# Dynamic convolution in a four-layer kernel: the orders of TensorE, VectorE and ScalarE laid out anew

## The chip, the cores and the metric

One core of one Trainium2 chip runs the whole program. The metric is the device time of one execution in microseconds (us), the median of three runs. The profile shows one further execution, with its own time.

## The reference

Four layers follow one another on `x` (16 samples, 64 channels, 64 x 64), each fed with a group-normalised copy and added to its input. Only the first is touched by the change, a dynamic convolution:

```python
g = jnp.mean(x, axis=(2, 3))
h = jax.nn.relu(g @ w1.T + b1)
alpha = jax.nn.softmax(h @ w2.T + b2, axis=-1)
weff = jnp.einsum('bk,koihw->boihw', alpha, experts)
beff = jnp.einsum('bk,ko->bo', alpha, bias)
...
x = x + _L0_conv_ref(_gn(x), ...)
x = x + _L1_conv_ref(_gn(x), ...)
x = x + _L2_conv_ref(_gn(x), ...)
x = x + _L3_conv_ref(_gn(x), ...)
```

Each sample has its own 3 x 3 weights: four experts mixed by a softmax over a small network of the sample's channel means. The other layers are two sets of directional sweeps and one attention with a local part.

## The kernel before

`dyn_conv` handles one sample after another. A sample lies in `raw` (four buffers) with image rows of even and odd number on the two halves of the partitions; it is convolved in four pieces (`CH` = 4) of 512 columns. For fp32 accuracy both operands are split into a high and a low part: `xz_hi`, `xz_lo` (two buffers each) and `w_hi`, `w_lo`. A piece is 18 products (L604): 12 of `xz_hi` with both weight parts, in two blocks of six (`products_high`), and six of `xz_lo` with `w_hi` (`products_low`). A sample has 72 products.

While sample n is convolved, the weights of sample n+1 are made, and the result of n-1 is normalised. Who does what:

- VectorE: `input_stats` (L662, four pieces), `aggregate` (L311, L668) and `squares` (L672 to L674) give the moments; `group_var` (L679 to L684, L348 to L350) turns the group mean that TensorE made into a variance and the first guess of its inverse root; `gate_mean` (L697), `gate_hidden` (L702), `softmax_in` (L707 to L709), `mixing_weights` (L713 to L715); `mix` (L720 for expert 0, L722 for the other three, L727 for the added input), `low_weights` (L731); `remainder` (L736), which makes a half of `xz_lo`; `result_stats` (L743) of each evacuated piece, `effective_bias` (L746 to L748) and `result_affine` (L691).
- ScalarE: `centre` (L525) makes a half of `xz_hi`, `evacuate` (L532) adds a finished piece to its bias and writes it to `raw`, `hidden` (L537), `exps` (L541), `high_weights` (L545), and `to_slot` (L551): two moves of a quarter of the normalised result into `S` a call.
- TensorE: besides the products, `group` (L589) averages moments over channel groups (for the input, INP, and the result, RES), `hid` (L593) and `logits` (L598) are the two layers of the small network.
- GpSimd: the inverse root, eleven small steps for the input and eleven for the result (`newton_rsqrt`). SyncE: loads of samples and stores of results; the load of sample n+4 waits for the store of n and its four moves to `S`.

The order on each engine is the order of the code in `sample` of that engine's block; nothing reorders it. An engine waits where its next instruction's semaphore is not there, and all behind it waits too. The waits that matter here:

```python
def products_high(n, q, u, blk):
    if blk == 0:
        if q == 0:
            pe.wait_ge(w_ready, n + 1)
```
```python
def group(n, c):
    pe.wait_ge(me_ready[c], n + 1)
```
```python
def gate_hidden(m):
    dve.wait_ge(h_ready, m + 1)
```

`w_ready` comes from `low_weights`, `me_ready` from `squares`, `h_ready` from `hidden`. `walk` runs `sample` for n = 0 and 1, a loop of three turns of four samples, and two more.

## Time and profile before

| what | value |
|---|---|
| median of 3 runs | 3129.11 us (3128.0 to 3129.72) |
| the profiled execution's own time | 3132.45 us |
| its span | 3130.7 us |
| busy: TensorE, VectorE, ScalarE, GpSimd | 88%, 69%, 44%, 9% |
| dynamic convolution | 0 to about 429 us of the span |

The shares are means over four layers. The change concerns the first 429 us alone, and only what is read there bears on it. The profile gives the time of every instruction, the granted clock of TensorE (1.0 is the full 2.4 GHz, 0.5 is 1.2 GHz), and what ended an engine's idle time. A time ahead of an instruction is its start in us from the span's start.

### The profile page before, as it was taken

The page shows a single profiled execution, that of the slowest core. Times are in us where ns is not written, and L with a number is a line of the kernel's source. Part 1 is how long each engine was busy: PE and PEld are TensorE (multiplying, and loading weights), DVE is VectorE, ACT ScalarE, POOL GpSimd, SP SyncE. Part 2 cuts the span into 40 slices and gives each one's busy share as a digit, 9 for nine tenths or more (in the row PEclk, how much of TensorE's full clock was granted, in tenths as well). Part 3 has the DMA queues.
Part 4 walks back from the last instruction along what each step waited for, and adds up shares of the span by engine and source line. Part 5 has one row for each costly group of instructions (what it writes and reads, how often), then busy time and mean ns, then how long its engine had stood idle before and what let it go on. Part 6 is the DMA issues. An engine that isn't in the chain of part 4 may idle for free. (4 is left out here: it accounts for less than half of the span.)

```text
span 3130.7 us, 71818 instructions
## 1 busy us (share of the span) xinstructions
PE 2747.3 (88%) x25712; PEld 2482.8 (79%) x25712; DVE 2172.1 (69%) x5174; ACT 1363.0 (44%) x2113; POOL 288.4 (9%) x801
## 2 busy tenths in 40 slices
PE   5888879999999999917969998878999999999791
PEld 3666669999999999913447777758999999999791
DVE  7888846666666666687018888886666666666865
ACT  3766642246632222236436666643225662222120
POOL 1112110000000000045000101010000000000602
PEclk9899989999999999958979999998999999999795
DMA  4334230000000000087054877856000000000758
GB/s 89 81 90 99 67 124 0 0 0 0 0 0 0 0 0 0 0 233 198 1 87 73 120 104 102 116 73 107 0 0 0 0 0 0 0 0 0 121 94 127
DMA packets 735622, 164.89 MB, mean 53 GB/s; under 512 B 728209, under 2 KB 728849, under 8 KB 730641
## 3 DMA queue, kind: packets, MB, share of 16 engines
q1 hardware_dynamic: 608928, 136.86, 22.7%
q10 hardware_dynamic: 126576, 26.41, 5.4%
q8 instruction: 81, 1.33, 0.2%
q14 instruction: 37, 0.30, 0.0%
HBM read 96.13 MB, written 67.11 MB: 52 GB/s over the span
## 5 line engine op out<-in xcount | busy, mean ns | idle before, releaser
L269 PE MATMUL L_conv<-L_x_hi,L_w_hi 128*128 128x256 f32 x5040 | 1251.0, 283 | 46.5 <-DVE L_w_lo L236 28.7
L269 PE MATMUL L_conv<-L_x_hi,L_w_lo 128*128 128x256 f32 x5040 | 1249.5, 283 | 0.0
L156 ACT ACTIVATE L_row_b<-S,L_bias 128x256 f32 (+1 forms) x1008 | 514.2, 510 | 1168.9 <-DVE L_x_hi L210 1158.0
L269 PEld LDWEIGHTS L_conv<-L_x_hi,L_w_hi 128*128 128x128 f32 x5040 | 958.7, 190 | 49.5 <-issue 28.9
L269 PEld LDWEIGHTS L_conv<-L_x_hi,L_w_lo 128*128 128x128 f32 x5040 | 957.0, 190 | 0.0
L220 DVE SCALAR_TENSOR_TENSOR S<-L_conv,L_neg_bias,L_row_b 128x256 f32 x1008 | 487.7, 484 | 517.5 <-PE L_conv L273 516.7
L273 PE MATMUL L_conv<-L_x_lo,L_w_hi 128*128 128x256 f32 x5040 | 771.3, 284 | 4.9 <-DVE L_x_lo L212 4.8
L273 PEld LDWEIGHTS L_conv<-L_x_lo,L_w_hi 128*128 128x128 f32 x5040 | 677.7, 190 | 7.4 <-DVE L_x_lo L212 7.4
L212 DVE TENSOR_TENSOR L_x_lo<-S,L_x_hi 128x256 fp32r<-128x256 f32 x1016 | 455.3, 448 | 34.7
L210 DVE TENSOR_SCALAR L_x_hi<-S 128x256 fp32r (+1 forms) x1016 | 316.7, 312 | 35.3
L604 PE MATMUL dc_conv<-dc_xz_hi,dc_w_hi 128*128 128x512 f32 x384 | 171.3, 446 | 6.5 <-DVE dc_w_lo L731 6.5
L604 PE MATMUL dc_conv<-dc_xz_hi,dc_w_lo 128*128 128x512 f32 x384 | 166.2, 433 | 0.0
L160 ACT COPY S<-S (+1 forms) x252 | 156.2, 620 | 7.3 <-DVE S L220 2.8
L1690 POOL TENSOR_TENSOR fs_buf<-fs_buf,S 128x1024 f32<-128x1024 f32 x21 | 67.8, 3267 | 888.5 <-DVE S L220 786.2
L551 ACT ACTIVATE S<-dc_raw,dc_small 64x1024 f32 (+1 forms) x62 | 133.7, 2156 | 7.9 <-DVE dc_small L691 6.7
L604 PE MATMUL dc_conv<-dc_xz_lo,dc_w_hi 128*128 128x512 f32 x384 | 103.2, 404 | 0.0
L604 PEld LDWEIGHTS dc_conv<-dc_xz_hi,dc_w_hi 128*128 128x128 f32 x384 | 79.8, 208 | 26.1 <-DVE dc_w_lo L731 6.6
L945 PE MATMUL lp_taps<-S,lp_band 128*128 128x256 f32 x256 | 90.3, 435 | 9.6 <-ACT S L912 9.6
L338 POOL TENSOR_TENSOR lp_sq_pool<-lp_guess 128x1 f32<-128x1 f32 x48 | 9.3, 193 | 955.6 <-DVE lp_guess L350 953.0
L604 PEld LDWEIGHTS dc_conv<-dc_xz_hi,dc_w_lo 128*128 128x128 f32 x384 | 80.3, 209 | 19.3
L604 PEld LDWEIGHTS dc_conv<-dc_xz_lo,dc_w_hi 128*128 128x128 f32 x384 | 74.6, 194 | 20.3
L918 ACT ACTIVATE S<-lp_taps,lp_lb 128x256 f32<-128x256 f32 x128 | 57.8, 475 | 71.0 <-PE lp_taps L947 71.0
(177 smaller groups left out, 2896.4 us busy)
## 6 DMA issues: line engine op xcount, KB each, us to landing
dc_raw<-x SPq DMA_DIRECT2D x32, 512.0 KB, 6.6
x_scratch<-dc_raw SPq DMA_DIRECT2D x16, 1024.0 KB, 7.4
lp_xr<-x_scratch SPq DMA_DIRECT2D x16, 1024.0 KB, 7.0
x_scratch<-lp_xr SPq DMA_DIRECT2D x32, 512.0 KB, 7.7
at_res<-x_scratch SPq DMA_DIRECT2D x32, 512.0 KB, 10.5
x_scratch<-at_res SPq DMA_DIRECT2D x64, 256.0 KB, 5.3
fs_buf<-x_scratch SPq DMA_DIRECT2D x32, 512.0 KB, 6.7
at_G<-x_scratch ACTq DMA_DIRECT2D x56, 256.0 KB, 5.8
```

Of the source, the lines that this page charges most:

```text
L156: nc.scalar.activation(row_b[p][:, :, :], line(k, at_step(k, i), p), ACT.Identity, bias=bias[:, k:k + 1]).then_inc(row_b_ready[p], 1)
L160: nc.scalar.copy(*quarter(hj, *QUARTERS[q])).then_inc(act_moved, 1)
L210: nc.vector.tensor_scalar(inner(x_hi[p]), row, 1.0, None, ALU.mult).then_inc(hi_ready[p], 1)
L212: nc.vector.tensor_tensor(inner(x_lo[p]), row, inner(x_hi[p]).bitcast(F32), ALU.subtract).then_inc(lo_ready[p], 1)
L220: nc.vector.scalar_tensor_tensor(out=row, in0=conv[p][:, 0:NB * J].rearrange("p (j b) -> p j b", b=NB), scalar=neg_bias[:, k:k + 1], in1=r ...
L269: nc.tensor.matmul(out, w[:, k, s * P:(s + 1) * P], x_hi[p][:, s:s + J, :], start=(s == 0 and n == 0), stop=False)
L273: mm = nc.tensor.matmul(out, w_hi[:, k, s * P:(s + 1) * P], x_lo[p][:, s:s + J, :], start=False, stop=(s == NBLK - 1))
L551: nc.scalar.activation(dst, src, ACT.Identity, bias=shift, scale=scale).then_inc(s_done, 1)
L604: mm = nc.tensor.matmul(conv[q][:, :], part[:, at:at + P], x[:, q * CB + blk:q * CB + blk + CB, dw:dw + W], start=(first and dw == j == 0) ...
L918: nc.scalar.activation(column(every, slice(0, J), w, p), taps[g % 4][:, 0:J * NB].rearrange("p (i b) -> p i b", b=NB), ACT.Identity, bias= ...
L945: nc.tensor.matmul(out, bands.band0[:, w, :], column(every, slice(0, J), w, p), start=True, stop=False)
L1690: return eng.tensor_tensor(buf[:, :, :], buf[:, :, :], columns_of(self.S, item % B)[:, :, self.columns(item)], ALU.add)
```

## The change

Four things are changed in `dyn_conv`.

1. TensorE: the group average of the next input stands behind the first piece of a sample and no longer ahead of it; `hid` and `logits` come later in the products.
2. VectorE: within a sample, `remainder` of the second half is made in the sample that uses it, right after `effective_bias`; `remainder` of the first half stands between `mixing_weights` and the mixing; `gate_hidden` follows `gate_mean`. `mix` of expert 0 leaves VectorE.
3. ScalarE: it scales expert 0 into PSUM (`first_expert`), `centre` of the second half comes ahead of `exps`, and the moves to `S` are spread singly, the fourth into the next sample.
4. The start: the first mixing precedes the statistics of the second input; the experts are loaded by SyncE behind sample 0. The end: VectorE makes three of the last sample's moves, ScalarE one.

The diff, cut to its core: first `sample` of TensorE, then that of VectorE with its start, then `first_expert` and `sample` of ScalarE.

```diff
             def sample(t, k):
...
-                if not last:
-                    group(n + 1, INP)
                 products_high(n, 0, u, 0)
                 products_high(n, 0, u, 1)
                 products_low(n, 0, u)
                 if not last:
-                    hid(n + 1)
+                    group(n + 1, INP)
                 products_high(n, 1, u, 0)
                 if not first:
                     group(n - 1, RES)
+                products_high(n, 1, u, 1)
+                if not last:
+                    hid(n + 1)
+                products_low(n, 1, u)
+                products_high(n, 2, u, 0)
                 if not last:
                     logits(n + 1)
-                products_high(n, 1, u, 1)
-                products_low(n, 1, u)
...
             def sample(t, k):
                 if not last:
                     group_var(n + 1, INP, k + 1)
+                effective_bias(k)
+                remainder(n, k, 1)
                 if not first:
                     result_stats(n * CH - 1, (k - 1) % PER, CH - 1)
-                effective_bias(k)
-                if not first:
                     aggregate("result", RES)
                     squares(RES)
                 if not last:
                     gate_mean(n + 1, k + 1)
-                    remainder(n + 1, k + 1, 0)
                     gate_hidden(n + 1)
                 if not first:
                     group_var(n - 1, RES, k - 1)
...
                 result_stats(n * CH, k % PER, 0)
                 if not last:
                     mixing_weights(n + 1)
-                    for e in range(KE):
-                        mix(n + 1, (k + 1) % 2, e)
+                    remainder(n + 1, k + 1, 0)
                 if not first:
                     result_affine(n - 1, k - 1)
+                if not last:
+                    for e in range(1, KE):
+                        mix(n + 1, (k + 1) % 2, e)
                 result_stats(n * CH + 1, k % PER, 1)
                 if not last:
-                    remainder(n + 1, k + 1, 1)
                     low_weights(n + 1, (k + 1) % 2)
...
             gate_hidden(0)
+            softmax_in(0)
+            mixing_weights(0)
+            dve.wait_ge(ex_in, 2 * 16)
+            for e in range(1, KE):
+                mix(0, 0, e)
+            low_weights(0, 0)
             remainder(0, 0, 0)
-            softmax_in(0)
-            remainder(0, 0, 1)
...
+            def first_expert(m): 
+                act.wait_ge(weight_ready, m + 1)
+                nc.scalar.activation(w_mix, ex[0], ACT.Identity, scale=weight[:, 0:1]).then_inc(first_mixed, 1)
...
             def sample(t, k):
                 if not first:
                     evacuate(n * CH - 1, (k - 1) % PER, CH - 1, n - 1)
+                if not first and not second:
+                    to_slot(n - 2, (k - 2) % PER, 1, 1)
                 if not last:
                     centre(t, k + 1, 0)
                 evacuate(n * CH, k % PER, 0, n)
                 if not last:
                     hidden(n + 1)
+                    centre(t, k + 1, 1)
                     exps(n + 1)
-                    centre(t, k + 1, 1)
+                    first_expert(n + 1)
                 evacuate(n * CH + 1, k % PER, 1, n)
+                if not first:
+                    to_slot(n - 1, (k - 1) % PER, 0, 0)
                 if not last:
                     high_weights(n + 1, (k + 1) % 2)
                 if not first:
-                    to_slot(n - 1, (k - 1) % PER, 0)
+                    to_slot(n - 1, (k - 1) % PER, 0, 1)
                 evacuate(n * CH + 2, k % PER, 2, n)
                 if not first:
-                    to_slot(n - 1, (k - 1) % PER, 1)
+                    to_slot(n - 1, (k - 1) % PER, 1, 0)
```

TensorE, sample 1, from the end of sample 0's products. Before (L604 are products, L589 `group`, L593 `hid`, L598 `logits`):

```order
L604 MATMUL dc_conv<-dc_xz_lo,dc_w_hi 128x512 x6
L589 MATMUL dc_group<-dc_small,dc_avg 128x2
L604 MATMUL dc_conv<-dc_xz_hi,dc_w_hi 128x512
...
L604 MATMUL dc_conv<-dc_xz_lo,dc_w_hi 128x512 x6
L593 MATMUL dc_gate<-dc_small,dc_w1s 32x1
L604 MATMUL dc_conv<-dc_xz_hi,dc_w_hi 128x512
...
L589 MATMUL dc_group<-dc_small,dc_avg 128x2
L598 MATMUL dc_gate<-dc_small,dc_ones 128x4
```

And with the change (L619 products, L604 `group`, L608 `hid`):

```order
L619 MATMUL dc_conv<-dc_xz_lo,dc_w_hi 128x512 x6
L619 MATMUL dc_conv<-dc_xz_hi,dc_w_hi 128x512
...
L619 MATMUL dc_conv<-dc_xz_lo,dc_w_hi 128x512 x6
L604 MATMUL dc_group<-dc_small,dc_avg 128x2
L619 MATMUL dc_conv<-dc_xz_hi,dc_w_hi 128x512
...
L604 MATMUL dc_group<-dc_small,dc_avg 128x2
L619 MATMUL dc_conv<-dc_xz_hi,dc_w_hi 128x512
...
L608 MATMUL dc_gate<-dc_small,dc_w1s 32x1
L619 MATMUL dc_conv<-dc_xz_lo,dc_w_hi 128x512 x6
```

The first `group` (the next input's) has moved behind a whole piece of 18 products; the second (the last result's) has stayed six products behind the first piece, and `hid` now comes six products after it and no longer ahead of it.

VectorE, from the last guess step of the input's `group_var` on. Before:

```order
L350 TENSOR_SCALAR dc_small<-dc_small 128x1
L743 BN_STATS dc_bn<-dc_raw 128x6
L746 TENSOR_TENSOR dc_small<-dc_small 128x4
...
L674 TENSOR_TENSOR dc_small<-dc_small 128x1
L697 TENSOR_SCALAR dc_small<-dc_small 128x1
L736 SCALAR_TENSOR_TENSOR dc_xz_lo<-dc_raw,dc_small,dc_xz_hi 64x17x64 x2
L702 TENSOR_SCALAR dc_small<-dc_small 32x4
L679 COPY dc_small<-dc_group 128x2
```

And with the change (L752 `remainder`, L759 `result_stats`, L691 the end of `squares`, L714 `gate_mean`, L719 `gate_hidden`):

```order
L764 TENSOR_TENSOR dc_small<-dc_small 128x1
L752 SCALAR_TENSOR_TENSOR dc_xz_lo<-dc_raw,dc_small,dc_xz_hi 64x15x64 x2
L759 BN_STATS dc_bn<-dc_raw 128x6
...
L691 TENSOR_TENSOR dc_small<-dc_small 128x1
L714 TENSOR_SCALAR dc_small<-dc_small 128x1
L719 TENSOR_SCALAR dc_small<-dc_small 32x4
L696 COPY dc_small<-dc_group 128x2
```

Two instructions of `remainder` now stand ahead of the result's statistics, and none between `gate_mean` and `gate_hidden`.

## Rows read from the trace of the kernel before

**Rows 1.** Busy time and granted clock in two stretches of the dynamic convolution (columns in the first line).

```profile
core 0: us, PE busy (x) PEld busy (x) DVE busy (x) ACT busy (x) POOL busy (x), PEclk, DMA share, GB/s
100.00:200.00 100.00, 83.88 (x332) 64.29 (x330) 84.68 (x220) 70.36 (x66) 18.70 (x96) 0.91 0.37 85
200.00:300.00 100.00, 81.01 (x321) 61.89 (x320) 84.90 (x227) 71.00 (x67) 18.68 (x96) 0.93 0.36 84
```

**Rows 2.** Waits of TensorE between 60 and 380 us: in total, times, longest.

```profile
PE dc_group L589 <- DVE dc_small L674: 39.4, 13, 3.3
```

**Rows 3.** The tile of the mixed weights: count, ns min/median/max, first and last start.

```profile
L545 ACT CAST dc_w_hi<-dc_mixed x16: 799/802/804, 34.3 to 388.9; 128x768 fp32r<-128x768 f32 x16
L731 DVE TENSOR_TENSOR dc_w_lo<-dc_mixed,dc_w_hi x16: 956/958/960, 35.1 to 392.0; 128x768 fp32r<-128x768 f32 x16
```

**Rows 4.** VectorE in order of time, 51 to 56 us (start, us, line, operation).

```profile
54.19 0.96 DVE L731 TENSOR_TENSOR dc_w_lo<-dc_mixed,dc_w_hi 128x768 fp32r<-128x768 f32 x1
```

**Rows 5.** VectorE in order of time, one sample of the loop.

```profile
149.66 0.96 DVE L731 TENSOR_TENSOR dc_w_lo<-dc_mixed,dc_w_hi 128x768 fp32r<-128x768 f32 x1
...
154.34 0.14 DVE L679 COPY dc_small<-dc_group 128x2 f32<-128x2 f32 x1
...
157.37 0.69 DVE L743 BATCH_NORM_STATS2 dc_bn<-dc_raw 128x6 f32<-128x512 f32 x1 [1.88 <-ACT dc_raw L532]
...
159.16 0.27 DVE L697 TENSOR_SCALAR dc_small<-dc_small 128x1 f32<-128x1 f32 x1
159.70 2.73 DVE L736 SCALAR_TENSOR_TENSOR dc_xz_lo<-dc_raw,dc_small,dc_xz_hi 64x1088 fp32r<-64x1088 f32 x2 [0.28 <-ACT dc_xz_hi L525]
...
163.81 0.15 DVE L707 TENSOR_TENSOR dc_small<-dc_gate,dc_small 128x4 f32<-128x4 f32 x1
...
165.57 1.02 DVE L720 TENSOR_SCALAR dc_mixed<-S,dc_small 128x768 f32<-128x768 f32 x1
166.63 3.14 DVE L722 SCALAR_TENSOR_TENSOR dc_mixed<-dc_ex,dc_small,dc_mixed 128x768 f32<-128x768 f32 x3
...
170.41 0.69 DVE L743 BATCH_NORM_STATS2 dc_bn<-dc_raw 128x6 f32<-128x512 f32 x1
171.01 2.44 DVE L736 SCALAR_TENSOR_TENSOR dc_xz_lo<-dc_raw,dc_small,dc_xz_hi 64x960 fp32r<-64x960 f32 x2
173.49 0.96 DVE L731 TENSOR_TENSOR dc_w_lo<-dc_mixed,dc_w_hi 128x768 fp32r<-128x768 f32 x1
```

**Rows 6.** TensorE in order of time, the same sample and the next one's head.

```profile
153.87 0.38 PE L589 MATMUL dc_group<-dc_small,dc_avg 128*128 128x2 f32 x2 [2.81 <-DVE dc_small L674]
...
166.00 0.40 PE L604 MATMUL dc_conv<-dc_xz_hi,dc_w_hi 128*128 128x512 f32 x1
...
170.28 0.40 PE L604 MATMUL dc_conv<-dc_xz_hi,dc_w_hi 128*128 128x512 f32 x1
...
177.69 0.59 PE L589 MATMUL dc_group<-dc_small,dc_avg 128*128 128x2 f32 x2 [2.96 <-DVE dc_small L674]
178.15 0.77 PE L604 MATMUL dc_conv<-dc_xz_hi,dc_w_hi 128*128 128x512 f32 x1
...
183.41 1.63 PE L604 MATMUL dc_conv<-dc_xz_lo,dc_w_hi 128*128 128x512 f32 x6
```

**Rows 7.** The start: hidden layer of the first sample.

```profile
17.87 0.26 PE L593 MATMUL dc_gate<-dc_small,dc_w1s 128*32 128x1 f32 x2 [4.96 <-DVE dc_small L697]
19.46 0.25 ACT L537 ACTIVATE dc_small<-dc_gate,dc_small 32x1 f32<-32x1 f32 x1
```

**Rows 8.** The end of the stage: last convolution, its evacuation, the last moves.

```profile
413.54 1.58 PE L604 MATMUL dc_conv<-dc_xz_lo,dc_w_hi 128*128 128x512 f32 x6
416.54 0.69 ACT L532 ACTIVATE dc_raw<-dc_conv,dc_small 128x512 f32<-128x512 f32 x1
423.91 4.24 ACT L551 ACTIVATE S<-dc_raw,dc_small 64x1024 f32<-64x1024 f32 x2 [6.68 <-DVE dc_small L691]
423.91 2.33 DVE L823 TENSOR_SCALAR S<-dc_raw,dc_small 64x1024 f32<-64x1024 f32 x2
```

More of the change, by code:

```diff
@@ L288 @@
 HID = 32
-PER_LOOP = 34
+PER_LOOP = 32
 PER = 4
@@ L384, in dyn_conv @@
     logit, prob, alpha, bprod = small[:, 20:24], small[:, 24:28], small[:, 28:32], small[:, 32:36]
-    top, total, beff, gmean = small[:, 36:37], small[:, 37:38], small[:, 38:39], small[:, 39:40]
+    top, total, gmean = small[:, 36:37], small[:, 37:38], small[:, 39:40]
+    beff = [small[:, 76 + u:77 + u] for u in range(2)]
     stat = [small[:, 40 + 4 * i:44 + 4 * i].rearrange("p (a b) -> p a b", a=2) for i in range(3)]
@@ L466, in store @@
                              raw[u][:, :, :].rearrange("p i w -> p (i w)")).then_inc(x1_stored, 16)
-            for n in range(PER):
+            load(0, 0)
+            sp.dma_start(ex[0], halves(experts[:, 0, :])).then_inc(ex_in, 16)
+            sp.dma_start(ex_rest[:, :, :], experts[:, 1:KE, :]).then_inc(ex_in, 16)
+            for n in range(1, PER):
                 load(n, n)
@@ L514, in _ @@
             act.dma_start(eye[:, :], identity).then_inc(consts_in, 16)
-            act.dma_start(ex[0], halves(experts[:, 0, :])).then_inc(ex_in, 16)
-            act.dma_start(ex_rest[:, :, :], experts[:, 1:KE, :]).then_inc(ex_in, 16)
             def centre(t, k, z):
@@ L555, in sample @@
                 first, last = isinstance(n, int) and n == 0, isinstance(n, int) and n == B - 1
+                second = isinstance(n, int) and n == 1
                 if not first:
                     evacuate(n * CH - 1, (k - 1) % PER, CH - 1, n - 1)
+                if not first and not second:
+                    to_slot(n - 2, (k - 2) % PER, 1, 1)
                 if not last:
@@ L576, in _ @@
             centre(0, 0, 0)
-            centre(0, 0, 1)
             hidden(0)
             exps(0)
+            act.wait_ge(ex_in, 2 * 16)
+            first_expert(0)
+            centre(0, 0, 1)
             high_weights(0, 0)
@@ L635, in sample @@
                     group(n - 1, RES)
+                products_high(n, 1, u, 1)
[3 more added lines that the diff above has]
+                products_high(n, 2, u, 0)
                 if not last:
                     logits(n + 1)
-                products_high(n, 1, u, 1)
-                products_low(n, 1, u)
-                for q in range(2, CH):
-                    products_high(n, q, u, 0)
-                    products_high(n, q, u, 1)
-                    products_low(n, q, u)
+                products_high(n, 2, u, 1)
+                products_low(n, 2, u)
+                products_high(n, 3, u, 0)
+                products_high(n, 3, u, 1)
+                products_low(n, 3, u)
             pe.wait_ge(consts_in, 9 * 16)
@@ L746, in effective_bias @@
                 chain.step(nc.vector.tensor_tensor(bprod, bks, alpha, ALU.mult))
-                chain.step(nc.vector.reduce_sum(beff, bprod, AX_X))
-                nc.vector.tensor_tensor(beff, beff, minus_mean[u % 2], ALU.subtract).then_inc(beff_ready, 1)
+                chain.step(nc.vector.reduce_sum(beff[u % 2], bprod, AX_X))
+                nc.vector.tensor_tensor(beff[u % 2], beff[u % 2], minus_mean[u % 2], ALU.subtract).then_inc(beff_ready, 1)
             def sample(t, k):
@@ L808, in _ @@
             squares(INP)
-            mixing_weights(0)
-            dve.wait_ge(ex_in, 2 * 16)
-            for e in range(KE):
-                mix(0, 0, e)
-            low_weights(0, 0)
             walk(dve, sample, chain, PER * PER_LOOP, marks)
@@ L820, in _ @@
             dve.wait_ge(affine_ready, B)
-            for pw in range(2):
-                dst, src, scale, shift = slot_move(B - 1, (B - 1) % PER, (B - 1) % 2, 1, pw)
+            for ph, pw in ((0, 1), (1, 0), (1, 1)):
+                dst, src, scale, shift = slot_move(B - 1, (B - 1) % PER, (B - 1) % 2, ph, pw)
                 nc.vector.tensor_scalar(dst, src, scale, shift, ALU.mult, ALU.add)
```

24 lines of the change are left out of this document (12 added, 12 removed).

## The prediction

> **What bounds the kernel now.** I read first how busy the engines are inside the stage, then who waits for whom, then one sample's order of time on VectorE and TensorE. No engine is full: in 100 us TensorE is busy 81 to 84, VectorE 85, ScalarE 71 [rows 1]. A sample takes 23.8 us: `low_weights` starts at 149.66 and again at 173.49 [rows 5]. That start is the clock I count samples by, because TensorE may not begin a sample without it. From the second sample's (54.19) to the last one's (392.03) there are 14 intervals, 24.13 us each on average [rows 3, 4]. A piece of 18 products takes 4.28 us (166.00 to 170.28), so 0.238 a product and 17.1 a sample [rows 6]; TensorE has some 6 us to spare in each.
>
> What spends the rest is a ring of small waits. The largest is at a sample's head: TensorE waits for the moments of the next input, 39.4 us in 13 waits, 3.0 each [rows 2]. The reader should see that this wait ends VectorE's work and does not delay it: VectorE takes up the answer at 154.34, 0.5 after the group product starts at 153.87 [rows 5, 6]. VectorE's own order (statistics, then the network, then the mixing, then `low_weights`) is what comes round every 23.8 us. The price of a pause in TensorE is the clock. After the pause that ends at 177.69, twelve products take 5.26 us (178.15 to 183.41) where twelve at full clock would take 12 x 0.238 = 2.86 [rows 6]: 2.4 us lost. The granted clock is 0.91 and 0.93 of full over 200 us [rows 1], so it is at 1.2 GHz for 18% and 14% of them, some 4 us a sample.
>
> **The change, part by part.** I walk one sample of the loop in the new order. T = 0 is the start of `low_weights`; durations are the old trace's, TensorE at full clock at first.
>
> 1. *Head.* `low_weights` is done at 1.0 [rows 3] and TensorE starts the first piece at once: its 3 us wait there is gone as a wait for moments. VectorE has the moments ready at 4.2 (149.66 to 153.87 [rows 5, 6]) and finishes one more `result_stats` (0.6, the step 170.41 to 171.01 [rows 5]) at 4.7. But the group product now stands behind the piece: 1.0 + 4.3 + 0.4 = 5.7. VectorE therefore waits 1.0 us, and all behind it is 1.0 later than before.
> 2. *VectorE to the result's moments.* `group_var` is seven small instructions, 1.15 us as an estimate from the pace of the small chains. Then `effective_bias`, a `result_stats`, aggregate and squares: 1.8 us in all (157.37 to 159.16 [rows 5]). Between them stands now half a `remainder`, 2.44 [rows 5], which before stood late in the sample. Result's moments: 5.75 + 1.15 + 1.8 + 2.45 = 11.15.
> 3. *TensorE meanwhile.* After the group product at 5.7 it has six products (1.43) and then needs just these moments: it stands from 7.1 to about 11.2. That is **a new pause of some 4.1 us in the middle of the sample**, longer than any at the head. Before, the moments were there in time.
> 4. *Network.* Six products, then `hid` at 12.8. ScalarE's `hidden` takes 0.25 [rows 7], with the hand-overs `gate_hidden` runs at 13.4. VectorE was ready for it since 11.4: a new wait of 2.0, where a `remainder` covered it before. VectorE does the result's `group_var` until 14.5. `logits` stands 12 products (2.86) behind `hid`: done at 16.2. VectorE waits 1.7 more.
> 5. *Softmax to mixing.* 163.81 to 165.57 gives 1.76 for softmax, one `result_stats` and the weights [rows 5]: 18.0. The first `remainder` takes 2.75 [rows 5]: 20.75. Under it ScalarE scales expert 0. No row shows ScalarE writing 768 columns to PSUM from SBUF; the cast of 768 columns takes 0.80 [rows 3] and VectorE's own scaling 1.02 (165.57) [rows 5]. I take 0.9; between these ends it costs nothing, since 2.75 us of `remainder` cover it, and without that cover it would cost its 0.9.
> 6. *Mixing to the end.* Three experts, the added input and `result_affine` go from 166.63 to 170.41, 3.8 [rows 5]; `result_stats` 0.6. The cast runs beside it. Next `low_weights`: 25.2.
>
> What VectorE gives up is 1.06 us (165.57 to 166.63 [rows 5]); what it gets are waits of 1.0, 2.0 and 1.7. It had waits of 1.88 and 0.28 [rows 5], now gone. So the period at full clock is 25.3 and not 23.8.
>
> *The clock.* TensorE now pauses 4.1 us in the middle and about 3 at the head. Most of the old 3 us pauses already brought the clock down for some 4 us. After the middle pause the slow products are no longer beside other work: `hid` stands six products behind it, `logits` twelve more, and VectorE waits for both. Twelve slow products are 12 x 0.19 = 2.3 us more: 27.6. When the head's pause also lowers the clock, the first piece, which VectorE now waits for, is longer: 9 to 18 slow products, 1.7 to 3.4. I count 1.7 in one sample of four, 0.4. **Period: 28.0.**
>
> Beside the rule of the skill: the Trainium skill's page Perfetto Trace Analysis, Matmul Optimizations, says TensorE's power scales with its utilisation, so matmuls should be issued back to back in batches. This case's trace agrees (0.91 and 0.93 granted in a stage with one such pause a sample), and by the rule two pauses a sample are worse than one.
>
> *Start.* `hid` of the first sample is done at 18.1 [rows 7]; ScalarE took it at 19.46 behind four `centre` instructions, now behind two, at once. Then `gate_hidden` and `logits` 0.8, softmax, exponential and weights 1.6, expert 0 0.9, mixing 3.65, cast 0.85: first `low_weights` at 26.35, not 35.1 [rows 3]: **-8.75**. But the first interval grows. Before it was 54.19 - 35.10 = 19.1 [rows 3, 4]. Now it holds a `remainder` (2.75) and the second input's statistics (3.3) as well; walked as above it is 24.5: **+5.4**. The experts behind sample 0 on SyncE's queue are needed at 20.8 only, and I cost their move at nothing.
>
> *Loads.* The fourth move, and so the load of n+4, comes some 6 us into the sample, the input is read at its end: I count nothing. If a load came late, VectorE's statistics would wait at a sample's end.
>
> *Loop.* 14 x (28.0 - 24.13) = **+54.2**.
>
> *End.* From the last `low_weights` (392.03) to the last products (413.54 + 1.58) it was 23.1 [rows 3, 8]; TensorE was behind then, and no longer is: 1 + 17.1 + about 2 for pause and clock = 20.1, -3.0. ScalarE came 1.4 late to the last piece (416.54 [rows 8]); in the new order it is free: -1.4. The last moves: 4.24 for two on ScalarE, now three of 1.17 on VectorE (2.33 for two) [rows 8]: 3.5, -0.7. **-5.1.**
>
> Sum: -8.75 + 5.4 + 54.2 - 5.1 = +45.8. The profiled execution took 3132.45; its sum is 3178. It stands 3.3 above the median of the runs shown, and against 3129.11 the same step gives **3175 us**.
>
> **The rivals.**
>
> *A. Faster: the head's wait is the bound.* If TensorE is what sets the pace, removing 3.0 us a sample pays in full: 14 x -3.0 = -42, with -8.75 + 0 - 5.1 beside it: 3073. For it speaks that this wait is the longest of TensorE's [rows 2] and that VectorE, the busiest with 85 [rows 1], loses 1.06. It decides by one point: the result's moments must be ready by 7.1, when TensorE needs them. By my walk they come at 11.2, 4.1 too late, so I give it little. The page Perfetto Trace Analysis of the Trainium skill, Optimizing Scalar/DVE Operations, speaks for the change here: with VectorE saturated, moving work to ScalarE may make sense. The trace has VectorE waiting in the chain, and by my walk waiting more.
>
> *B. The order costs its waits, but the clock holds.* Period 25.4: 14 x 1.27 = 17.8, so 3129 - 8.75 + 5.4 + 17.8 - 5.1 = 3138. Against it: pauses shorter than the new one lowered the clock already [rows 6].
>
> *C. Both pauses lower it in every sample.* Period 27.6 + 1.7 = 29.3: 14 x 5.17 = 72.4, so 3193.
>
> *D. Nothing measurable.* The parts cancel, or VectorE finds its waits elsewhere: 3129. It would need a period of 24.7.
>
> **How the numbers follow.** A measurement of this kernel tells about 0.2% (6 us) from no change. Forecast 0.70, C 0.14, B 0.08, A 0.05, D 0.03. The forecast's own spread is one microsecond of the period either way, 14 us. Forecast and C hold 0.84, so the range goes from 3150 (a period of 26.2) to 3198. Expert 0's bounds (0.8 to 1.02) change nothing in it. Slower by over 0.2%: 0.70 + 0.14 + 0.08 = 0.92. Within: 0.03. Faster: 0.05.
>
> **What would show it.** In the new profile: TensorE's `group` of the result waits about 4 us for `squares`, once a sample; `gate_hidden` waits 2 us or more for `hidden`; the sums of the softmax wait for `logits`; the granted clock of the stage falls below 0.9; `low_weights` first starts near 26 and then comes every 27.4 to 29.4 us; the next layer's first work starts near 475 and not 429. It is wrong if `group` of the result does not wait, or if the period is under 24.1.

## The result and the profile after

The change makes the kernel slower: 3209.39 us (median of 4 runs, 3202.43 to 3214.91) against 3129.41 (4 runs, 3128.0 to 3131.0) measured beside it; the ratio is 1.0245, 95% interval 1.0228 to 1.0263. That is 80 us. The forecast was 46 us slower (3175); its range ended at 3198, 11 us short. The profiled execution took 3208.35 us, with a span of 3206.5, 75.8 more than before.

First the two stretches of [rows 1] again, in the changed kernel:

```profile
core 0: us, PE busy (x) PEld busy (x) DVE busy (x) ACT busy (x) POOL busy (x), PEclk, DMA share, GB/s
100.00:200.00 100.00, 78.11 (x274) 57.81 (x274) 63.83 (x175) 58.40 (x58) 21.70 (x84) 0.83 0.28 70
200.00:300.00 100.00, 73.96 (x268) 54.97 (x267) 69.10 (x178) 62.46 (x57) 19.42 (x72) 0.85 0.27 63
```

VectorE has fallen from 85 to 64 and 69: it waits. TensorE is busy for 74 to 78 us in which it does 274 and 268 instructions (332 and 321 before), because the granted clock is 0.83 and 0.85. Who waits for whom between 60 and 440 us (in total, times, longest; [rows 2] has TensorE's longest wait in the kernel before):

```profile
ACT dc_small L540 <- PE dc_gate L608: 71.9, 13, 5.8
...
PE dc_group L604 <- DVE dc_small L691: 55.6, 13, 5.3
...
DVE dc_small L719 <- ACT dc_small L540: 38.1, 13, 2.9
PE dc_conv L619 <- DVE dc_w_lo L747: 36.7, 12, 3.2
DVE dc_small L724 <- PE dc_gate L613: 34.3, 13, 3.2
DVE dc_small L696 <- PE dc_group L604: 32.5, 12, 3.6
```

TensorE stands twice in each sample: 4.3 us for `squares` of the result (L691, the new pause) and 3.1 for `low_weights` (L747). VectorE stands three times: 2.7 for the group product (L696), 2.9 for `hidden` (L719), 2.6 for `logits` (L724). The tile of the low weights, with first and last start, answers to [rows 3]:

```profile
L747 DVE TENSOR_TENSOR dc_w_lo<-dc_mixed,dc_w_hi x16: 956/958/959, 26.4 to 475.1; 128x768 fp32r<-128x768 f32 x16
```

One sample on VectorE, to be set beside [rows 5]:

```profile
234.57 0.96 DVE L747 TENSOR_TENSOR dc_w_lo<-dc_mixed,dc_w_hi 128x768 fp32r<-128x768 f32 x1
...
241.88 0.16 DVE L696 COPY dc_small<-dc_group 128x2 f32<-128x2 f32 x1 [2.56 <-PE dc_group L604]
...
243.45 2.46 DVE L752 SCALAR_TENSOR_TENSOR dc_xz_lo<-dc_raw,dc_small,dc_xz_hi 64x960 fp32r<-64x960 f32 x2
...
248.17 0.27 DVE L714 TENSOR_SCALAR dc_small<-dc_small 128x1 f32<-128x1 f32 x1 [0.72 <-POOL dc_small L343]
...
251.38 0.22 DVE L719 TENSOR_SCALAR dc_small<-dc_small 32x4 f32<-32x4 f32 x1 [2.94 <-ACT dc_small L540]
...
255.20 0.16 DVE L724 TENSOR_TENSOR dc_small<-dc_gate,dc_small 128x4 f32<-128x4 f32 x1 [2.58 <-PE dc_gate L613]
...
256.83 2.73 DVE L752 SCALAR_TENSOR_TENSOR dc_xz_lo<-dc_raw,dc_small,dc_xz_hi 64x1088 fp32r<-64x1088 f32 x2
...
264.32 0.96 DVE L747 TENSOR_TENSOR dc_w_lo<-dc_mixed,dc_w_hi 128x768 fp32r<-128x768 f32 x1
```

And TensorE, beside [rows 6]:

```profile
235.76 0.79 PE L619 MATMUL dc_conv<-dc_xz_hi,dc_w_hi 128*128 128x512 f32 x1 [3.22 <-DVE dc_w_lo L747]
236.35 0.63 PE L619 MATMUL dc_conv<-dc_xz_hi,dc_w_lo 128*128 128x512 f32 x1
...
241.57 0.28 PE L604 MATMUL dc_group<-dc_small,dc_avg 128*128 128x2 f32 x2
...
247.50 0.59 PE L604 MATMUL dc_group<-dc_small,dc_avg 128*128 128x2 f32 x2 [4.11 <-DVE dc_small L691]
247.96 0.77 PE L619 MATMUL dc_conv<-dc_xz_hi,dc_w_hi 128*128 128x512 f32 x1
...
250.79 0.27 PE L608 MATMUL dc_gate<-dc_small,dc_w1s 128*32 128x1 f32 x2
...
254.78 0.38 PE L613 MATMUL dc_gate<-dc_small,dc_ones 32*128 32x4 f32 x2
```

Products of 0.63 us instead of 0.40 mark the low level of the clock (1.2 GHz). They stand behind both pauses, and so in front of everything VectorE waits for: the input's group product (241.57), `hid` (250.79) and `logits` (254.78). The sample took 29.75 us. The next layer's first work started at 507.2, not near 475 as forecast, and `low_weights` came every 30.05 us on the mean, above the 27.4 to 29.4 of the forecast.

Split as the prediction split it, with the starts of `low_weights` as marks:

| term | forecast | measured |
|---|---|---|
| start (first `low_weights`) | -8.75 | 26.40 - 35.10 = -8.7 |
| first interval | +5.4 | (54.44 - 26.40) - 19.09 = +8.95 |
| 14 intervals | 14 x (28.0 - 24.13) = +54.2 | 14 x (30.05 - 24.13) = +82.9 |
| end | -5.1 | (507.2 - 475.1) - 37.2 = -5.1 |
| sum | +45.8 | +78.0 (the later layers give back 2) |

### The profile page after: what moved, and what is told of

Same layout as the page of the kernel before. It is cut to its first block and busy times, and to the rows that moved or that the text cites. A ratio compares the mean times of both kernels' runs of the same rounds, so it can differ in the third digit from the quotient of the medians.

```text
span 3206.5 us, 71795 instructions
## 1 busy us (share of the span) xinstructions
PE 2781.3 (87%) x25712; PEld 2497.0 (78%) x25712; DVE 2159.3 (67%) x5159; ACT 1378.5 (43%) x2128; POOL 316.1 (10%) x801
## 5 line engine op out<-in xcount | busy, mean ns | idle before, releaser
L619 PE MATMUL dc_conv<-dc_xz_hi,dc_w_hi 128*128 128x512 f32 x384 | 183.4, 478 | 53.3 <-DVE dc_w_lo L747 53.3
L619 PE MATMUL dc_conv<-dc_xz_hi,dc_w_lo 128*128 128x512 f32 x384 | 175.6, 457 | 0.0
L619 PEld LDWEIGHTS dc_conv<-dc_xz_hi,dc_w_hi 128*128 128x128 f32 x384 | 86.4, 225 | 80.3 <-issue 41.9
L619 PE MATMUL dc_conv<-dc_xz_lo,dc_w_hi 128*128 128x512 f32 x384 | 117.2, 446 | 0.0
L619 PEld LDWEIGHTS dc_conv<-dc_xz_hi,dc_w_lo 128*128 128x128 f32 x384 | 86.7, 226 | 20.0
L619 PEld LDWEIGHTS dc_conv<-dc_xz_lo,dc_w_hi 128*128 128x128 f32 x384 | 81.9, 218 | 21.2
```

What stands on the lines that cost most here:

```text
L619: mm = nc.tensor.matmul(conv[q][:, :], part[:, at:at + P], x[:, q * CB + blk:q * CB + blk + CB, dw:dw + W], start=(first and dw == j == 0) ...
```

## The experiments

My theory was that TensorE's group products are asked for in the wrong place, that the pauses which follow cost the clock, and that the rest of the change is free. The rivals: the clock is not the cause of the missed part; or the other parts (ScalarE's expert, the halves of `remainder`, the new start) cost the time themselves. All figures of a period below are means over the same 14 intervals of one trace; before it is 24.13, after 30.05. Each ratio is against the kernel before as measured beside that run (3131.65 us for e1 to e4, 3134.69 for e5 to e8, 3128.99 for e9 to e11, 3129.64 for e12).

**e1: the changed kernel with TensorE's order of before.**

```diff
+                if not last:
+                    group(n + 1, INP)
                 products_high(n, 0, u, 0)
                 products_high(n, 0, u, 1)
                 products_low(n, 0, u)
                 if not last:
-                    group(n + 1, INP)
+                    hid(n + 1)
                 products_high(n, 1, u, 0)
                 if not first:
                     group(n - 1, RES)
-                products_high(n, 1, u, 1)
-                if not last:
-                    hid(n + 1)
-                products_low(n, 1, u)
-                products_high(n, 2, u, 0)
                 if not last:
                     logits(n + 1)
```

> The changed kernel with TensorE's order of before (the next input's group product at a sample's head, hid behind the first piece, logits inside the second); VectorE and ScalarE keep the new order. Theory (the group products are asked for at the wrong place: the input's behind a whole piece, the result's ahead of its moments): the input's group product no longer delays VectorE by 2.6 us a sample; TensorE then waits at the head again, but VectorE has 1.06 us less to do. Period near 23 us instead of 30, total 3095 to 3125, at or below before's 3129. Rival (VectorE's new order, with a remainder half ahead of the result's moments and nothing between gate_mean and gate_hidden, is what costs): period stays above 27, total above 3170.

Measured: 3139.75 us (10 runs), ratio 1.0025 (1.0009 to 1.004), period 25.39. TensorE's order of before takes back 70 of the 80 us, with VectorE's new order kept. The time stays 15 us above the theory's range, and the period did not fall under that of before: VectorE still waits for TensorE and GpSimd (2.57 for the result's group product, 1.17 and 0.70 for GpSimd in the sample at 205.36).

**e2: the kernel before with TensorE's new order alone** (the same lines the other way round).

> The kernel before with TensorE's new order alone. Theory: the input's group product behind the first piece delays VectorE's group_var by 1 us at full clock and by 2.5 when the first piece is slow, and the result's moments are late by the same; pauses in mid sample lower the clock. Period 26 to 28, total 3165 to 3190. Rival (VectorE's order is what costs): TensorE's order alone costs under 10 us, total below 3140.

Measured: 3171.65 us, ratio 1.0131 (1.0098 to 1.0164), period 26.36. As the theory has it. It costs 40 us beside VectorE's old order and 70 beside the new one: the two orders make each other worse, so neither has a cost of its own apart from the other.

**e3: the changed kernel, with the half `remainder` that stood ahead of the result's moments put between `gate_mean` and `gate_hidden`.**

```diff
                 effective_bias(k)
-                remainder(n, k, 1)
                 if not first:
                     result_stats(n * CH - 1, (k - 1) % PER, CH - 1)
                     aggregate("result", RES)
                     squares(RES)
                 if not last:
                     gate_mean(n + 1, k + 1)
+                remainder(n, k, 1)
+                if not last:
                     gate_hidden(n + 1)
```

> The changed kernel with one move on VectorE: the second half of remainder stands between gate_mean and gate_hidden instead of ahead of the result's statistics. The result's moments come 2.45 us earlier and the wait for hidden is covered. Theory: the pause in mid sample falls from 4.1 to about 1.7 us, the clock stays up behind it, hid and logits come earlier by 2.45 plus some 2.5 of slow products: period 25.5 to 26.5, total 3140 to 3165. Rival (the head's pause alone makes the clock and the time): only the covered wait is won, 2.9 us or less a sample and no clock, total 3170 to 3190.

Measured: 3156.55 us, ratio 1.0071 (1.0046 to 1.0096), period 26.80: 3.25 a sample from one move of 2.44 us of work. `group` of the result now waits 23.3 us in 14 waits, 1.7 each and not 4.3, and the same `remainder` covers the wait for `hidden`. The time is in the theory's range, the period 0.3 above it, for one part of the theory did not hold: the clock did not stay up. It is low for 6.34 us a sample (9.75 in the changed kernel). Behind the shortened middle pause it fell in only four of the 14 samples, but the head's pause grew to 3.6 us (50.5 us in 14 waits for L747), and the clock fell there in every sample.

**e4, e5, e6: the clock.** The changed kernel with products whose result is thrown away, issued where TensorE would stand: in both pauses (e4), at the head only (e5: 11 and 0), in the middle only (e6: 0 and 16).

```diff
+            def filler(n, q, u, count):
+                pe.wait_ge(hi_ready, n * 4 + 4)
+                pe.wait_ge(evac_done, n * CH + (q + 1 - CH))
+                for i in range(count):
+                    nc.tensor.matmul(conv[q][:, :], w_hi[1 - u][:, 0:P], xz_hi[u][:, q * CB:q * CB + CB, 0:W], start=True, stop=True)
...
+                if not first:
+                    filler(n, 0, u, 11)
                 products_high(n, 0, u, 0)
...
                 if not first:
+                    filler(n, 2, u, 16)
                     group(n - 1, RES)
```

> The changed kernel with TensorE kept busy by throw-away products of 512 columns: 11 ahead of a sample's first piece and 16 ahead of the result's group product, written to banks that the next piece clears. They lie inside the pauses of 3.0 and 4.1 us at full clock. Theory (2.0 us a sample of the loss over my forecast, and some 4.3 in all, are the lowered clock): granted clock at 1.0 in the loop, period 25.3 to 26.3, total 3140 to 3160. Rival (the clock does not matter, the waits themselves are longer than I walked): the period stays within 1 us of 30, total above 3190.

> The changed kernel with eleven throw-away products on TensorE ahead of each sample's first piece, in the pause at the sample's head only; the pause in the middle stays as it is. Nothing of the result is changed. With throw-away products in both pauses the period fell from 30.05 to 26.48 us. Theory (each pause costs its own stretch of slow products, and both stand in the chain): the head's share is the smaller one, about 1.6 us of 3.6, since the group product of the next input stands behind 18 products of which some 8 to 9 are slow (0.19 us more each); period 28.3 to 28.9, time 3182 to 3192. Rival (the two are one effect: the clock lost at the head only moves the middle's pause, which then decides alone): no change from 3209, at least 3203. Second rival (the head's pause is the cause of both, since a sample that is late at the head makes the middle's pause): near 3164.

> The changed kernel with sixteen throw-away products on TensorE ahead of the group product of the result, in the middle pause only; the pause at the head stays. Nothing of the result is changed. Theory (each pause costs its own stretch): the middle's share is 2.0 to 2.5 us of 3.6, since the hidden layer's product stands six and the logits twelve more products behind it; period 27.6 to 28.1, time 3170 to 3183. Rival (one pause is the cause of the whole loss): 3164 or lower here and no change with the head's alone, or no change here. If the gains of this kernel and of the one with the head's products add up to the 45 us of both together, within 8 us, the two stretches are separate terms, as the prediction had them, and only their sizes were off.

The last column is the time that the clock spent at its low level in the 14 intervals, a sample.

| kernel | us | ratio (95%) | period | low clock, us a sample |
|---|---|---|---|---|
| before | 3129.41 | | 24.13 | 3.66 |
| changed | 3209.39 | 1.0245 (1.0228 to 1.0263) | 30.05 | 9.75 |
| e5, head | 3185.4 | 1.016 (1.0133 to 1.0188) | 28.45 | 5.36 |
| e6, middle | 3189.95 | 1.016 (1.0128 to 1.0192) | 27.97 | 4.14 |
| e4, both | 3164.16 | 1.0091 (1.0061 to 1.0121) | 26.48 | 0.24 |

The stage of e4, in the columns of the first view:

```profile
100.00:200.00 100.00, 95.18 (x400) 72.08 (x399) 75.60 (x198) 69.00 (x63) 23.57 (x84) 0.99 0.32 76
```

The clock is nearly full, and TensorE does more (useless) work in less time. The head's pause costs 30.05 - 28.45 = 1.60 us a sample, the middle's 30.05 - 27.97 = 2.08; together 3.68, where both at once give 30.05 - 26.48 = 3.57. So they are separate terms that add: the clock is 14 x 3.6 = 50 us in the loop, of the 80. The whole stage says nearly the same: it ends at 507.2 in the changed kernel, at 485.7 in e5, 484.6 in e6 and 460.0 in e4, so 21.5 and 22.7 us for one pause and 47.3 for both. (e6 gives 6 of its loop's 29 us back at the stage's start and end. The ratios put 48 us on both.) None of the rivals came: neither run left the time where it was, and neither alone reached e4's. The times of e4 and e6 came 4 and 7 us above their ranges, the periods within them but for 0.2. What is left, 26.48 against 24.13, is the order; it is the least that the order costs, since the kernel before, too, has its clock low for 3.66 us a sample, and no run filled its pauses.

**e7: the new parts in the old order.** ScalarE's expert and order, the new start and end, half a `remainder` between the mixing weights and the mixing; but TensorE's sample as before and VectorE's nearly so.

```diff
                 if not last:
                     group_var(n + 1, INP, k + 1)
-                effective_bias(k)
-                remainder(n, k, 1)
                 if not first:
                     result_stats(n * CH - 1, (k - 1) % PER, CH - 1)
+                effective_bias(k)
+                if not first:
                     aggregate("result", RES)
                     squares(RES)
                 if not last:
                     gate_mean(n + 1, k + 1)
+                    remainder(n + 1, k + 1, 0)
                     gate_hidden(n + 1)
...
                     mixing_weights(n + 1)
-                    remainder(n + 1, k + 1, 0)
+                    remainder(n + 1, k + 1, 1)
```

> The changed kernel's new parts (expert 0 scaled by ScalarE, ScalarE's new order, half a remainder between the mixing weights and the mixing, the mixing of the first sample ahead of the second input, the new end), but within a sample the order of TensorE before the change and, but for the remainder's other half staying ahead of the hidden layer's gate, the order of VectorE before it. Theory (the order of the group products costs the time; the parts are free or gain a little): the start's 8.75 and the end's 5 us are kept, expert 0 off VectorE takes up to 1.06 us from a period of 24.1, less a wait for ScalarE; against this the first interval grows by some 5. Time 3100 to 3130. Rival (scaling on ScalarE with the remainder over it is itself a loss, for instance since the remainder slows GpSimd's small steps and delays the gates): 3140 or more.

Measured: 3130.27 us (10 runs), ratio 0.9989 (0.9976 to 1.0003): no difference, at the upper edge of the theory. First `low_weights` -8.1, first interval +7.7, end -5.3, loop 14 x (24.51 - 24.13) = +5.3: sum -0.4. Together the parts cost nothing and bring nothing in this order. That is a sum, and no run here parts it: VectorE has 1.06 us less to do in each sample, and yet the loop's period is 0.38 longer. Two of its waits between 60 and 440 us show where some of it went:

```profile
DVE dc_small L711 <- POOL dc_small L343: 21.4, 16, 3.3
DVE dc_small L717 <- POOL dc_small L343: 21.3, 14, 1.6
```

In each sample VectorE waits 1.5 us for GpSimd's inverse root of the input (L717) and about 1.1 for that of the result (L711); in the kernel before it waited for GpSimd in three samples of the loop only, and instead for ScalarE's evacuation. At the result's root `remainder` runs beside GpSimd and makes two steps slow (1.04 and 1.18 us at 217.04 and 218.16, not 0.19; the last section shows the like). That is what e7's rival had named; its loss is just not larger than what the parts bring.

**e8: an order in which TensorE's requests are met.** VectorE finishes the result's moments right after the input's variance; TensorE asks for the input's moments at the head, as before the change, and for the result's behind the first twelve products.

```diff
             def sample(t, k):
+                if not last:
+                    group(n + 1, INP)
                 products_high(n, 0, u, 0)
                 products_high(n, 0, u, 1)
+                if not first:
+                    group(n - 1, RES)
                 products_low(n, 0, u)
                 if not last:
-                    group(n + 1, INP)
+                    hid(n + 1)
                 products_high(n, 1, u, 0)
...
                 if not last:
                     group_var(n + 1, INP, k + 1)
-                effective_bias(k)
-                remainder(n, k, 1)
                 if not first:
                     result_stats(n * CH - 1, (k - 1) % PER, CH - 1)
                     aggregate("result", RES)
                     squares(RES)
+                effective_bias(k)
+                if not first:
+                    group_var(n - 1, RES, k - 1)
                 if not last:
                     gate_mean(n + 1, k + 1)
+                    remainder(n + 1, k + 1, 0)
                     gate_hidden(n + 1)
```

(`logits` stands six products behind `hid`, `softmax_in` behind the next `result_stats`, the other half `remainder` covers expert 0, and on ScalarE two moves change places with their neighbours.)

> A version meant to beat both kernels: the new parts, with TensorE's group products of the input at a sample's head as before the change and the result's after the first twelve products, three products ahead of the hidden layer's; VectorE takes a result_stats and the aggregate and squares of the result right after the input's variance, ahead of effective_bias, so that the result's moments are there when TensorE comes to them; one remainder half covers the hidden layer, the other expert 0's scaling. Theory: no wait for TensorE's group of the result, period 23.0 to 23.8, start and end gained as in the changed kernel; 3095 to 3120. Rival (VectorE's own work with its small hand-overs fills the period, so no order of TensorE can go under that of the kernel before): 3125 to 3140.

Measured: 3099.22 us (4 runs, 3098.67 to 3102.42), ratio 0.9881 (0.9855 to 0.9908): faster than the kernel before by 1.2%, and than the changed one by some 3.5%. Twelve of the 14 intervals are 21.5 to 21.7 us, two are 25.5 and 24.2; mean 22.02, better than the theory's 23.0 to 23.8. VectorE's waits between 60 and 360 us are now these:

```profile
DVE dc_small L699 <- issue: 5.2, 2, 2.6
DVE dc_small L733 <- ACT dc_small L544: 5.1, 14, 0.4
DVE dc_small L717 <- POOL dc_small L343: 3.3, 13, 0.3
DVE dc_small L727 <- PE dc_gate L616: 1.2, 1, 1.2
```

Nothing of a microsecond a sample is left: VectorE's own work sets the pace, which e10 and e12 test. TensorE's pause at the head has shrunk too:

```profile
213.01 0.38 PE L607 MATMUL dc_group<-dc_small,dc_avg 128*128 128x2 f32 x2 [1.38 <-DVE dc_small L694]
```

The products behind it take 0.40, and the granted clock is 0.97 and 0.98 over the two stretches: it was low in the two late intervals only, 0.73 us a sample on the mean.

**e9 and e11: what the new start is worth.** e9 is e8 with the start of before (on ScalarE too, where all of `centre` comes ahead of `hidden`); e11 is e8 with the second input's statistics ahead of the first input's `remainder`.

```diff
             gate_hidden(0)
+            remainder(0, 0, 0)
             softmax_in(0)
-            mixing_weights(0)
-            dve.wait_ge(ex_in, 2 * 16)
-            for e in range(1, KE):
-                mix(0, 0, e)
-            low_weights(0, 0)
-            remainder(0, 0, 0)
             remainder(0, 0, 1)
             for q in range(CH):
                 input_stats(0, 1, q)
             aggregate("input", INP)
             squares(INP)
+            mixing_weights(0)
+            dve.wait_ge(ex_in, 2 * 16)
+            for e in range(1, KE):
+                mix(0, 0, e)
+            low_weights(0, 0)
```

> The version that beat both kernels, with the start of the kernel before: the second input's statistics and both remainder halves ahead of the first mixing, all four centre instructions ahead of the hidden layer; the loop and the end are not touched. Theory (what the new start gains is given back at once in the first interval, since the same VectorE work stands there instead): first low_weights near 35, the second one at 53.5 to 56 as with the new start (54.1), time within 5 us of it, 3095 to 3104. Rival (the new start's 8.7 us count): 3105 to 3110, second low_weights near 62.

> The version that beat both kernels, with one move in the start: behind the first low_weights VectorE takes the second input's statistics ahead of the first input's two remainder halves, so that TensorE has the group product, and with it its first piece, 5.2 us earlier. Theory (in the first interval VectorE's own line of work holds the end, and TensorE only its hidden layer's product): first interval 25.5 to 27, time 3097 to 3100, hardly to be told from 3099. Rival (the first interval is TensorE's): first interval 22.5, time 3093 to 3095.

Measured: e9 3097.39 us, ratio 0.9906 (0.9877 to 0.9936); e11 3096.62, ratio 0.9886 (0.9865 to 0.9907): neither is to be told from e8. The second `low_weights` starts at 53.5 with the old start, 54.1 with the new, 52.7 in e11. Mixing for sample 0 first is a gain of 8.4 us that the first interval takes back whole (27.65 in e8, 18.65 in e9).

**e10 and e12: what expert 0 on ScalarE is worth.** e10 is e8 with the scaling on VectorE.

```diff
-                if e == 1:
-                    dve.wait_ge(first_mixed, m + 1)
-                chain.step(nc.vector.scalar_tensor_tensor(out=w_mix, in0=ex[e], scalar=weight[:, e:e + 1],
-                                                          in1=w_mix, op0=ALU.mult, op1=ALU.add))
+                if e == 0:
+                    chain.step(nc.vector.tensor_scalar(w_mix, ex[0], weight[:, 0:1], None, ALU.mult))
+                else:
+                    chain.step(nc.vector.scalar_tensor_tensor(out=w_mix, in0=ex[e], scalar=weight[:, e:e + 1],
+                                                              in1=w_mix, op0=ALU.mult, op1=ALU.add))
```

> The version that beat both kernels, with expert 0 scaled by VectorE again (tensor_scalar ahead of the three other experts, as in the kernel before); nothing else moves. Theory (in this order VectorE sets the pace, with hardly a wait in its sample, so its 1.06 us count in full): period 21.5 becomes 22.6, 15 samples, time 3112 to 3118. Rival (the scaling is hidden behind another engine in any order): no change, 3097 to 3103.

Measured: 3130.81 us (10 runs), ratio 0.9998 (0.9987 to 1.0008), period 24.17. Both sides missed: 1.06 us of work cost 2.15. Where the rest went, TensorE's rows and VectorE's waits of e10 say:

```profile
154.61 0.38 PE L598 MATMUL dc_group<-dc_small,dc_avg 128*128 128x2 f32 x2 [2.70 <-DVE dc_small L685]
```

```profile
DVE dc_small L690 <- PE dc_group L598: 17.4, 12, 2.5
```

The pause at the head is 2.70 us instead of 1.38; the granted clock in the two stretches is 0.93 and 0.91; and VectorE, which hardly waited in e8, now waits for the result's group product. That stands behind twelve products which take 4.4 us here (154.86 to 159.30) and 2.9 at full clock; eight of them are slow. e12 tests that: e10 with nine throw-away products at the head.

> The version with expert 0 on VectorE in the new order (period 24.17 us where the expert's own 1.06 us would have made it 22.6 from 21.5), with nine throw-away products on TensorE in the pause at a sample's head; nothing of the result is changed. Theory (the 1.06 us lengthen TensorE's pause at the head from 1.4 to 2.7 us, which brings the clock down, and the result's group product, which stands behind twelve slow products, then holds VectorE up by 1.3 to 2.5 us): with the pause filled the granted clock stays at 1.0, VectorE's wait for the result's group product goes, period 22.5 to 23.1, time 3108 to 3118. Rival (the scaling on VectorE costs more than its duration for another reason, such as what ScalarE and GpSimd now do beside it): period near 24.2, 3126 or more.

Measured: 3114.91 us, ratio 0.9948 (0.9927 to 0.9969), period 23.12, and of the same views as before:

```profile
100.00:200.00 100.00, 90.29 (x382) 67.58 (x381) 89.25 (x236) 73.02 (x70) 26.67 (x97) 1.00 0.36 85
200.00:300.00 100.00, 90.89 (x380) 67.55 (x378) 89.10 (x236) 73.05 (x71) 31.70 (x113) 0.98 0.36 86
```

With the clock held, the expert costs 23.12 - 22.02 = 1.10, about its own duration (1.2 against e9's loop, which is e8's with the clock never low: 21.90). The other 24.17 - 23.12 = 1.05 were the clock's. The period came 0.02 above the theory's range, the time within it.

## Why the prediction was wrong

The direction and the mechanism were right: the chance of 0.92 for slower rested on a walk of one sample whose waits all appeared. Forecast and measured, VectorE at the group product 1.0 and 2.56, at `hidden` 2.0 and 2.94, at `logits` 1.7 and 2.58; TensorE's new pause 4.1 and 4.11 (from 8.8 to 12.9 in the sample at 234.57, not from 7.1 to 11.2: the slow first piece moved both ends alike). The start's -8.75 and the end's -5.1 came to 0.1. First `low_weights` was to start near 26, and did at 26.4; the granted clock was to fall below 0.9, and did. Expert 0 on ScalarE took 0.91 against the 0.9 taken, hidden as said. What failed were sizes in two terms of the sum, and both erred the same way: even rival C, with 29.3 a sample, was under the measured 30.05.

**The loop, 28.0 against 30.05.** Three parts, by e4 to e6:

- *The head's pause.* The prediction counted its clock as "1.7 in one sample of four, 0.4". It lowered the clock in 13 of 14 samples, and cost 1.60 in each on the mean. This is the largest miss, 1.2 of 2.05, 17 us over the loop. The trace of before spoke against the choice: there pauses of 3.0 lowered the clock in ten of 14 samples, "most", as the text itself says. I had priced the same pause as common in the old order and rare in the new one. What made it matter was rightly seen, that VectorE now waits behind the first piece. Rival C, given 0.14, had it in every sample and 3193.
- *The middle's pause.* 2.3 forecast, 2.08 measured.
- *The walk at full clock.* 25.3 against e4's 26.48. In e4's sample at 214.47 each step is late by a little more: the input's group product at 5.57 (forecast 1.0 + 4.3 = 5.3), `gate_hidden` 13.89 (13.4), the first step of `softmax_in` 16.98 (16.2), next `low_weights` 26.1 (25.2 by the walk). They look like hand-overs of 0.1 to 0.2 us that I had left out; no run takes them apart. The last 0.4 is of another kind: the walk is that of a typical sample, and I set it against a mean, 24.13, that holds two late intervals (25.6 and 25.7 before).

1.2 - 0.2 + 1.2 = 2.2 for the 2.05 missed.

**The first interval, 24.5 against 28.0.** Its two largest waits on VectorE in the changed kernel:

```profile
40.05 0.27 DVE L714 TENSOR_SCALAR dc_small<-dc_small 128x1 f32<-128x1 f32 x1 [2.25 <-POOL dc_small L343]
...
45.50 0.16 DVE L724 TENSOR_TENSOR dc_small<-dc_gate,dc_small 128x4 f32<-128x4 f32 x1 [4.36 <-PE dc_gate L613]
```

The first is GpSimd's inverse root, late by 1.8 because of the `remainder` beside it (last section); the prediction had put nothing for that. TensorE stood 3.69 us for `hid` meanwhile, and the clock fell: the twelve products up to `logits` took 4.6 us (40.53 to 45.09) and not 2.9, which is 1.7 of the second wait. 1.8 + 1.7 make the 3.5 missed. Sample 0 was walked as a sample of the loop, and both were left out of it.

The Trainium skill's page Perfetto Trace Analysis, Matmul Optimizations, asks for matmuls back to back, since the engine's power scales with its utilisation. The runs agree: e4 to e6 put 3.6 us a sample on the two pauses. The same page of the Trainium skill, Optimizing Scalar/DVE Operations, says that with VectorE saturated, moving work to ScalarE may make sense. In e8's order, where VectorE is the bound, expert 0 on ScalarE was worth 2.15 us a sample, half of it by the clock (e10, e12); in the old order the parts together brought nothing, and the move alone wasn't run (e7).

## What to carry to other kernels

Walk one period in the new order and ask for each product that another engine needs: which work now stands ahead of it, and is its operand ready when its engine comes to it? Price a pause of TensorE by the slow products that stand between it and the next hand-over, in every period, as soon as the old trace shows the clock falling after pauses of that length. Moving work off the busiest engine may bring nothing while that engine waits in each period (e7, with other parts beside it). Where it no longer waits, it paid double here, since a shorter period also shortened the other engine's pause (e10, e12).

## What the runs showed of the hardware

**VectorE's `remainder` holds GpSimd.** Four steps of the inverse root on GpSimd in the changed kernel, beside VectorE's `remainder` at 243.45 (two instructions, 2.46 us together, shown above):

```profile
243.13 0.19 POOL L338 TENSOR_TENSOR dc_small<-dc_small 128x1 f32<-128x1 f32 x1 [16.55 <-DVE dc_small L350]
243.41 0.19 POOL L339 TENSOR_TENSOR dc_small<-dc_small 128x1 f32<-128x1 f32 x1
243.68 1.03 POOL L340 TENSOR_TENSOR dc_small<-dc_small 128x1 f32<-128x1 f32 x1
244.79 1.18 POOL L342 TENSOR_TENSOR dc_small<-dc_small 128x1 f32<-128x1 f32 x1
```

A step takes 0.19. The last two shown end at 244.71 and 245.97, where the two VectorE instructions end (244.66 and 245.91): a step that starts under `remainder` runs until that VectorE instruction is over, and the next one meets the second instruction. The inverse root, which is twelve such steps and not the eleven named ahead of the prediction, is late by 1.8 here. In the trace of before none of 384 such steps met a `remainder`; 42 met the three experts' mixing, and took 0.191 on the mean. In the changed kernel 45 met a `remainder` and took 0.80 on the mean. The Trainium skill's page SBUF — State Buffer, SBUF: two separate sides, says that a VectorE operation with two inputs in SBUF and a GpSimd operation that reads SBUF share a port pair: the one that starts first holds it for its whole instruction, and the other is blocked. The trace agrees: `remainder` reads `raw` and `xz_hi`, both in SBUF; the mixing has one operand in PSUM. Shape differs too, and no run parts the two. In the loop of the changed kernel VectorE waits 0.7 us a sample for it, and waits 2.9 more for `hidden` right behind; in its first sample, in e1 (0.70 for the input's root and 1.17 for the result's in the sample shown) and at the result's root in e7 (1.1) VectorE waits for it too. No run takes the effect away by itself, so what it costs in time is not shown.

**Pauses and the clock.** With one pause of 2.7 us a sample (e10) the granted clock fell in 13 of the 14 samples, 3.66 us a sample on the mean. With one of 1.38 (e8) it did not fall in twelve of the 14; it fell in the two late ones, where a second pause stands behind the first (1.37 at 165.96, 2.44 at 171.82), 0.73 on the mean. What the low level costs is less than the time at it would suggest: 3.4 us less of it a sample gave 1.05 us in e10, and 9.5 less gave 3.6 in the changed kernel.

**The loop's turns.** Two of the 15 intervals, the 7th and the 11th, are late in ten of the 14 kernels: 25.5 and 24.2 among 21.5 in e8, 25.2 and 25.2 among 22.8 in e12. In e8 VectorE waits up to 2.6 us for "issue" (for nothing that the profile shows) twice, in e12 up to 2.3. The two are four apart, as the turns of the loop are. In the changed kernel, e2, e3 and e6 they don't stand out. The cause beyond that row wasn't tried.
